# A recurrent chain of 16 chunks written out in full, with part of its VectorE work given to ScalarE

## What is computed

```
def step(M, chunk):                       # 64 tokens; 16 chunks one after the other
    eta, alpha = ...                      # means over the chunk of sigmoids
    outputs = einsum('bci,boi->bco', chunk, M)
    k_mean = (chunk / norm(chunk)).mean(axis=1)
    v_target = value_gen(outputs).mean(axis=1)
    err = v_target - einsum('boi,bi->bo', M, k_mean)
    M_new = alpha * M + eta * err[:, :, None] * k_mean[:, None, :]
    M_new = gate * M_new + (1 - gate) * M
    scale = minimum(30 / (norm(M_new) + 1e-6), 1)
    return M_new * scale, outputs
final_out = value_gen(outs)               # value_gen(y) = silu(y @ vg_w1.T) @ vg_w2.T + y
```

## Time and profile before

| | us |
|---|---|
| runs before: median of 3 (lowest to highest) | 1191.34 (1190.2 to 1191.75) |
| the profiled execution: its own time | 1186.12 |
| the profiled execution: its span, first to last instruction | 1184.1 |
| of this, from the chain's first product to the transposes after it | 909.21 to 998.88, 89.7 |
| one chunk in the chain, between the states of chunks 0 and 14 | 77.06 / 14 = 5.50 |

### The profile page before, as it was taken

One profiled execution on the slowest core, in us unless ns is written; L12 is line 12 of the kernel. 1 busy time (PEld: TensorE's weight loads), 2 busy tenths in 40 slices (PEclk: granted clock), 3 DMA queues, 4 the chain that ended last, 5 costly groups with the idle time before them and its releaser, 6 DMA issues.

```text
span 1184.1 us, 20954 instructions
## 1 busy us (share of the span) xinstructions
PE 1063.8 (90%) x5294; PEld 707.9 (60%) x5326; DVE 881.7 (74%) x2121; ACT 813.5 (69%) x1285; POOL 231.0 (20%) x328
## 2 busy tenths in 40 slices
PE   5638999999998559999999999999989888799997
PEld 2212222222322538888888888888868776677876
DVE  5863444334344669999999999999987888779997
ACT  5437999999998337777877787778762332256664
POOL 8454445445444200000000000000004111100000
PEclk9768999999999889999999999999997999699999
DMA  3455666666665137666666666676620000043231
GB/s 96 115 163 156 203 205 212 214 198 206 221 200 192 29 118 287 233 249 231 248 239 243 242 231 253 230 251 232 244 76 1 0 0 0 1 136 109 91 111 35
DMA packets 92907, 192.46 MB, mean 163 GB/s; under 512 B 9672, under 2 KB 56392, under 8 KB 82632
## 3 DMA queue, kind: packets, MB, share of 16 engines
q1 hardware_dynamic: 92880, 192.15, 48.0%
HBM read 154.03 MB, written 38.08 MB: 162 GB/s over the span
## 4 chain that ended last, share of the span: by engine, by line
PE 75%; DVE 13%; issue 4%; ACT 4%; POOL 2%; DMA 2%; DVEq 0%; ACTq 0%; SPq 0%; POOLq 0%
PE bank L1154 25%; PE bank L1167 14%; PE bank L1024 9%; PE bank L1161 8%; PE bank L1006 6%; PE bank L1009 5%; ACT ring L803 2%; PE bank L1035 1%; DVE state L1656 1%; PE bank L1255 1%; DVE ring L1396 1%; DVE xn L1346 1%; DMA ring<-c_rows 1%; DVE stats L1334 1%; PE bank L927 1%
## 5 line engine op out<-in xcount | busy, mean ns | idle before, releaser
L803 ACT ACTIVATE ring<-bank,minus_bound 128x1024 f32<-128x1024 f32 x256 | 271.3, 1111 | 30.8 <-PE bank L1009 13.5
L1154 PE MATMUL bank<-xh,w_parts 128*128 128x512 f32 x896 | 277.2, 391 | 1.9 <-DVEq L1554 1.9
L859 ACT ACTIVATE bank<-bank 128x512 f32<-128x512 f32 x320 | 186.2, 582 | 90.9 <-PE bank L1154 90.9
L1568 DVE TENSOR_TENSOR bank<-bank,ring 128x512 f32<-128x512 f32 x320 | 223.9, 700 | 29.5 <-DMA ring<-c_rows 6.6
L1167 PE MATMUL bank<-hh,w_parts 128*128 128x512 f32 x776 | 239.7, 390 | 0.0
L1560 DVE TENSOR_TENSOR hl<-bank,hh 128x512 fp32r<-128x512 f32 x321 | 218.6, 681 | 0.1
L1429 DVE TENSOR_TENSOR bank<-bank,corner 128x128 f32<-128x128 f32 x256 | 76.6, 299 | 174.4 <-PE bank L1009 145.7
L853 ACT ACTIVATE hh<-bank 128x512 fp32r<-128x512 f32 x321 | 190.4, 593 | 3.1 <-DVE bank L1568 3.0
L1154 PEld LDWEIGHTS bank<-xh,w_parts 128*128 128x128 f32 x896 | 168.0, 188 | 37.9 <-DVEq L1554 2.3
L1154 PE MATMUL bank<-xl,w_parts 128*128 128x512 f32 x448 | 174.7, 390 | 0.0
L1167 PEld LDWEIGHTS bank<-hh,w_parts 128*128 128x128 f32 x776 | 145.9, 188 | 30.7 <-ACT hh L853 0.4
(11 more groups left out here) (263 smaller groups left out, 1252.4 us busy)
## 6 DMA issues: line engine op xcount, KB each, us to landing
ring<-c_rows SPq DMA_DIRECT2D x80, 1024.0 KB, 5.1
w_parts<-w_pairs SPq DMA_DIRECT2D x160, 128.0 KB, 2.5
w_pairs<-xh SPq DMA_DIRECT2D x16, 768.0 KB, 4.4
q_stack<-q_parts SPq DMA_DIRECT2D x64, 144.0 KB
k_stack<-k_parts SPq DMA_DIRECT2D x64, 144.0 KB
w_pairs<-xl SPq DMA_DIRECT2D x16, 512.0 KB, 3.6
ring<-c_rows SPq DMA_DIRECT2D x16, 512.0 KB, 4.7
big<-in_w_exp SPq DMA_DIRECT2D x16, 384.0 KB, 4.8
```

Source lines behind the costliest of these rows:

```text
L803: act.activation(ring[:, c % RING * S:(c % RING + 1) * S], wide[c % 2][:], ACT.Exp, bias=minus_bound[:]).then_inc(exp_done, 1)
L859: act.activation(bank(4 + c % ZB), bank(4 + c % ZB), ACT.Silu).then_inc(silu_ready, 1)
L1154: ins = pe.matmul(out_, w[i], x_[j], start=start and k == 0, stop=stop and k == 2, skip_group_check=not start)
L1568: dve.tensor_tensor(bank(4 + c % ZB), bank(4 + c % ZB), cb[u][:, g * GW:(g + 1) * GW], ALU.mult).then_inc(hid_ready, 1)
```

## The change

All four loops are written out chunk by chunk, so that waits are on constants. Beside that:

- The decayed state `kept[b] = state[b] * steps[...]` is made by ACT, not by DVE, for chunk n + 1 at the end of chunk n. For chunk 0 it is made right after `steps_ready`.
- The sum of squares of batch 0 is made by ACT (`Square`), that of batch 1 stays on DVE. PE's sum waits for both.
- DVE makes both states directly after one another. Before, batch 0's squares stood between them.
- The second part of the outputs is copied out of PSUM by ACT, to `out_sum`. DVE adds the linear part and writes `memT` itself (`take_out`), and it does so for chunk n - 1 after the copy of the norm's sum in chunk n. ACT's copy to `memT` is gone.
- POOL's copy of `steps` is gone; PE and DVE read `steps`.
- Two spare products stand in each chunk, not four.
- In the last chunk the error products, the new state and its squares are left out, since nothing reads them.

```diff
-            with pool.Fori(0, NCH // 2) as i:
-                for u in range(2):
-                    n = i * 2 + u
-                    free(pool, err_psum[0], n, 1)
-                    free(pool, err_psum[1], n, 1)
-                    pool.tensor_copy(step[u][:], steps_flat[:, bass.ds(i * (2 * B * 3) + u * (B * 3), B * 3)])\
-                        .then_inc(step_ready, 1)
-                    ready(pool, norm_sq, n)
-                    pool.tensor_tensor(m_norm[:, 2, :], m_norm[:, 1, :], root[:, 0:B], ALU.pow).then_inc(norm_ready, 1)
+            for n in range(NCH):
+                pool.wait_ge(norm_sq, n + 1)
+                pool.tensor_tensor(m_norm[:, 2, :], m_norm[:, 1, :], root[:, 0:B], ALU.pow).then_inc(norm_ready, 1)
...
+            act.wait_ge(steps_ready, 1)
-            with act.Fori(0, NCH // 2) as i:
-                for u in range(2):
-                    n = i * 2 + u
-                    ready(act, scale_ready, n)
-                    for b in range(B):
-                        ready(act, mz_psum[b], n)
-                        act.activation(silu_z[b][:], bank(b)[:, 0:CH], ACT.Silu, scale=m_norm[:, 3, b:b + 1],
-                                       accum_out=h_sum[b][:]).then_inc(mz_silu[b], 1)
-                    for b in range(B):
-                        ready(act, out_taken[b], n)
-                        act.activation(memT[:, bass.ds(i * (2 * CH) + (b * S + u * CH), CH)], out_sum[b][:],
-                                       ACT.Copy).then_inc(out_copied[b], 1)
+                act.activation(kept[b], state[b][:], ACT.Copy, scale=steps[:, 0, b, 0:1]).then_inc(side_ready, 1)
+            for n in range(NCH):
+                act.wait_ge(scale_ready, n + 1)
+                for b in range(B):
+                    act.wait_ge(mz_psum[b], n + 1)
+                    act.activation(silu_z[b][:], bank(b)[:, 0:CH], ACT.Silu, scale=m_norm[:, 3, b:b + 1],
+                                   accum_out=h_sum[b][:]).then_inc(mz_silu[b], 1)
+                if n < NCH - 1:
+                    act.wait_ge(state_ready[0], n + 1)
+                    act.activation(m_sq[:, 0, :], state[0][:, 0:D], ACT.Square, accum_out=m_norm[:, 0, 0:1]).then_inc(side_ready, 1)
+                for b in range(B):
+                    act.wait_ge(out_psum[b], n + 1)
+                    act.activation(out_sum[b][:], bank(4 + b)[:, CH:2 * CH], ACT.Copy).then_inc(side_ready, 1)
+                for b in range(B if n < NCH - 1 else 0):
+                    act.wait_ge(state_ready[b], n + 1)
+                    act.activation(kept[b], state[b][:], ACT.Copy, scale=steps[:, n + 1, b, 0:1]).then_inc(side_ready, 1)
...
-                    free(pe, rows_ready, n, 1)
-                    pe.matmul(bank(6)[:, 256:256 + B], ones[:], m_norm[:, 0, :], start=True, stop=True).then_inc(norm_psum, 1)
-                    ready(pe, step_ready, n)
-                    for b in range(B):
-                        pe.matmul(bank(2 + b)[:, 0:2 * D], across(step[u][:, 3 * b + 2:3 * b + 3], P), state[b][:],
-                                  start=True, stop=True).then_inc(old_psum[b], 1)
-                    for b in range(B):
-                        free(pe, out_taken[b], n, 1)
-                        pe.matmul(bank(4 + b)[:, 0:CH], state[b][:, 0:D], chunk[b], start=True, stop=True)
-                    spare(7, 4)
-                    for b in range(B):
-                        ready(pe, mz_silu[b], n)
...
+                if n:
+                    pe.wait_ge(rows_ready, n)
+                    pe.wait_ge(side_ready, B + 5 * (n - 1) + 1)
+                pe.matmul(bank(6)[:, 256:256 + B], ones[:], m_norm[:, 0, :], start=True, stop=True).then_inc(norm_psum, 1)
+                for b in range(B):
+                    pe.matmul(bank(2 + b)[:, 0:2 * D], across(steps[:, n, b, 2:3], P), state[b][:],
+                              start=True, stop=True).then_inc(old_psum[b], 1)
+                for b in range(B):
+                    if n:
+                        pe.wait_ge(out_taken[b], n)
+                    pe.matmul(bank(4 + b)[:, 0:CH], state[b][:, 0:D], chunk[b], start=True, stop=True)
+                spare(7, 2)
+                for b in range(B):
+                    pe.wait_ge(mz_silu[b], n + 1)
+                    if n < NCH - 1:
...
-                ready(pe, out_copied[b], NCH - 1)
+                pe.wait_ge(out_taken[b], NCH)
...
-                    ready(dve, norm_psum, n)
-                    dve.tensor_copy(m_norm[:, 1, :], bank(6)[:, 256:256 + B]).then_inc(norm_sq, 1)
-                    ready(dve, step_ready, n)
-                    for b in range(B):
-                        link.sign(dve.tensor_scalar(kept[b], state[b][:], step[u][:, 3 * b:3 * b + 1], None, ALU.mult))
-                    link.wait()
-                    for b in range(B):
-                        ready(dve, old_psum[b], n)
-                        link.sign(dve.scalar_tensor_tensor(kept[b], bank(2 + b)[:, 0:2 * D], step[u][:, 3 * b + 1:3 * b + 2],
-                                                           kept[b], ALU.mult, ALU.add))
-                        if b == 0:
...
+            def take_out(n):
+                for b in range(B):
+                    dve.wait_ge(side_ready, B + 5 * n + (2 if n < NCH - 1 else 1) + b)
+                    dve.scalar_tensor_tensor(memT[:, b * S + n * CH:b * S + (n + 1) * CH], bank(4 + b)[:, 0:CH], m_norm[:, 3, b:b + 1],
+                                             out_sum[b][:], ALU.mult, ALU.add).then_inc(out_taken[b], 1)
+            for n in range(NCH):
+                dve.wait_ge(norm_psum, n + 1)
+                dve.tensor_copy(m_norm[:, 1, :], bank(6)[:, 256:256 + B]).then_inc(norm_sq, 1)
+                if n:
+                    take_out(n - 1)
+                for b in range(B):
+                    dve.wait_ge(old_psum[b], n + 1)
+                    dve.wait_ge(side_ready, 5 * n + b + 1)
+                    link.sign(dve.scalar_tensor_tensor(kept[b], bank(2 + b)[:, 0:2 * D], steps[:, n, b, 1:2], kept[b], ALU.mult, ALU.add))
+                    if b == 0:
+                        dve.wait_ge(norm_ready, n + 1)
+                        if n:
+                            dve.wait_ge(out_taken[0], n)
+                            dve.wait_ge(out_taken[1], n)
+                        link(dve.tensor_scalar(m_norm[:, 3, :], m_norm[:, 2, :], 1e-6, None, ALU.add))
+                        link(dve.reciprocal(m_norm[:, 3, :], m_norm[:, 3, :]))
+                        dve.tensor_scalar(m_norm[:, 3, :], m_norm[:, 3, :], MAX_NORM, 1.0, ALU.mult, ALU.min)\
+                            .then_inc(scale_ready, 1)
+                link.wait()
+                dve.wait_ge(scale_ready, n + 1)
+                if n < NCH - 1:
                     for b in range(B):
                         link.sign(dve.tensor_scalar(kept[b], kept[b], m_norm[:, 3, b:b + 1], None, ALU.mult))
                     link.wait()
                     for b in range(B):
-                        ready(dve, err_psum[b], n)
-                        dve.scalar_tensor_tensor(state[b][:], bank(6 + b)[:, 0:2 * D], step[u][:, 3 * b + 1:3 * b + 2],
+                        dve.wait_ge(err_psum[b], n + 1)
+                        dve.scalar_tensor_tensor(state[b][:], bank(6 + b)[:, 0:2 * D], steps[:, n, b, 1:2],
                                                  kept[b], ALU.mult, ALU.add).then_inc(state_ready[b], 1)
-                        ready(dve, state_ready[b], n)
-                        ins = dve.tensor_tensor_reduce(m_sq[:, b, :], state[b][:, 0:D], state[b][:, 0:D], 1.0, 0.0,
-                                                       ALU.mult, ALU.add, m_norm[:, 0, b:b + 1])
-                        if b == B - 1:
-                            ins.then_inc(rows_ready, 1)
-                    for b in range(B):
-                        ready(dve, out_psum[b], n)
-                        free(dve, out_copied[b], n, 1)
-                        link(dve.tensor_copy(out_sum[b][:], bank(4 + b)[:, CH:2 * CH]))
-                        dve.scalar_tensor_tensor(out_sum[b][:], bank(4 + b)[:, 0:CH], m_norm[:, 3, b:b + 1], out_sum[b][:],
-                                                 ALU.mult, ALU.add).then_inc(out_taken[b], 1)
-                assert link.n - first == per_turn, (link.n - first, per_turn)
-            link.end_loop(NCH // 2, per_turn)
+                    dve.wait_ge(state_ready[1], n + 1)
+                    dve.tensor_tensor_reduce(m_sq[:, 1, :], state[1][:, 0:D], state[1][:, 0:D], 1.0, 0.0,
+                                             ALU.mult, ALU.add, m_norm[:, 0, 1:2]).then_inc(rows_ready, 1)
+            take_out(NCH - 1)
```

More of the change, by code:

```diff
@@ L355, in build @@
         fold_ready = sem("fold_ready")
-        step_ready = sem("step_ready")
+        side_ready = sem("side_ready")
         state_ready = [sem(f"state_ready{b}") for b in range(B)]
@@ L362, in build @@
         scale_ready = sem("scale_ready")
```

(13 more changed lines are left out.)

40 lines of the change are left out of this document (4 added, 36 removed).

## The result

| | before | after |
|---|---|---|
| median of 4 runs each, us (lowest to highest) | 1190.77 (1188.25 to 1191.75) | 1172.24 (1167.51 to 1173.16) |
| the profiled execution: own time, span | 1186.12, 1184.1 | 1171.71, 1170.0 |

The ratio is 0.984, with a 95% interval of 0.9808 to 0.9871: the changed kernel is 18.5 us faster. The forecast was 1180.3 with a range of 1176 to 1187. Its sign was right and its size was not: 8.1 us too little, and the range missed the time. Of the 8.1, 7.5 are the gain (18.5 where 11.0 was forecast); the rest is the median of before, 1190.77 here and 1191.34 in the forecast.

A forecast was written before the change was run, and what follows sets the result against it. VectorE's gapless list (3.48 us) plus silu and product (1.87) bound each chunk. Fourteen chunks at 0.61 less give 8.6 us, the end 2.4, together 11.0; 1175.1 against the profiled execution, 1180.3 as a median, range 1176 to 1187.

The forecast's parts named there:

- the scale's first step, T+3.02: In each chunk, T being batch 0's state start: scale starts at T+3.02 through sum, copy and root; chunk 4.89 us.
- State 1 at T+0.50: Batch 1's state waits for its error product, about 0.5 us after the first pair, so starts at T+0.50, not T+0.73.
- The norm's copy 0.55 behind the sum: VectorE's copy of the norm's sum starts 0.55 us after PE's sum, at T+1.94; bounds 0.37 and 0.75.
- The root, 0.23 and 0.73, and the link of 0.12 to VectorE: POOL's root starts 0.23 us after the copy, takes 0.73, and VectorE follows 0.12 later (0 to 0.15).
- The other path, T+2.83: PE's old products, first there at T+2.43, then VectorE's addition: the scale's first step could start at T+2.83.
- The low end, 4.70: Shortest chunk, with sum, copy and root links short and old products deciding: 2.83 + 1.87 = 4.70 us, 11.2 us gained.
- Chunk 0, nothing is gained: First chunk: PE works off eight spare products until 909.4 us, sum, root and scale follow as before; no gain.
- The end, T+5.9: Last chunk: transposes start 5.9 us after state 14 instead of 8.32, a gain of 2.4 us.
- a gain behind the chain: Rival: PE's clock stands better behind the chain after a shorter end, 2 to 4 us more gained, 1177 us; chance 0.04.
- ScalarE's queue decides: Rival: ScalarE's operations run longer, `kept[0]` comes at T+2.83, chunk 5.1 us, time 1183.5 us; chance 0.09.
- PE's clock falls: Rival: with two fewer spare products PE's clock drops, low chunks 2.0 us longer, 1196 us with eight; chance 0.06.
- Code must be fetched: Rival: fetching the code of 16 written-out chunks stalls the chain, four stalls costing 7 us, 1187 us; chance 0.05.

The follow-up runs named there:

- the version with the outputs' part alone: Changed kernel with the decayed state and both squares back on VectorE, outputs done the new way: 5.497 us per chunk mean, thirteen at 5.39, one at 6.87.

## Why the prediction was right in kind and short in size

The step that failed is the sum of links up to the scale's first step, T+3.02. It came at T+2.65, which makes the chunk 4.52 us and not 4.89, 5.1 us over fourteen chunks. Two terms that were put at nothing, chunk 0 and the stretch behind the chain, gave 0.6 and 1.0 more, and the end 0.4.

- *VectorE's list sets the chunk, and what leaves it counts in full, until something else comes last*: right. Of the 0.98 (5.504 less 4.524), the decayed state is worth 0.53 and the square 0.34. The remaining 0.11 is what writing out the loop gives, and the outputs' part adds nothing to it.
- *State 1 at T+0.50*: it came at T+0.40 (two states in 0.88 us, each 0.48). I had read the distance of the error products' pairs; at full clock the second pair is there before VectorE has done the first state.
- *Squares and sum, T+1.39*: T+1.26. Of the 0.13 less, 0.10 is the state's and 0.03 the step's own.
- *The norm's copy 0.55 behind the sum*: 0.42 here. This is the largest mis-sized link, 0.13. The row that I leaned on, chunk 0 before, was taken with the clock at 0.50 for part of the time, and its sum took 0.53 instead of 0.38. At clock 1.00, chunk 0 of the changed kernel shows 0.44 (913.81 to 914.25). Among my bounds the low one, 0.37, was the nearer.
- *The root, 0.23 and 0.73, and the link of 0.12 to VectorE*: 0.24, 0.69 and 0.04. I had read 0.15 off a row where VectorE was busy with its own list, and had said so; I should have let that doubt pull the value down.
- *The other path, T+2.83*: the first addition came at T+2.22 and not T+2.43, the scale's step 0.43 behind it. In the changed kernel it stands right behind VectorE's two outputs; with these ahead of the copy it waited for the product and came at T+2.22 all the same, so the product too was there 0.21 earlier than I had it, 0.13 of that from the sum. Nor was there the wait for POOL that I had named as a sign: VectorE has no gap ahead of the scale's first step, only the one ahead of the norm's copy. Thus both paths came out at T+2.65, not T+3.02 and T+2.83, and the sum of the small differences is the 0.37 by which the chunk is shorter than forecast: 0.10 + 0.03 + 0.13 + 0.03 (the root) + 0.08 (the link). Times 14, that is 5.1 of the missing 7.2 us (18.2 less 11.0).
- *The last leg, 1.87 us*: 1.87 (937.83 to 939.70).
- *The low end, 4.70*: it took only the sum, copy and root links at their short ends. The old products' path, left at its middle, then decided. The state's step, common to both, had no bound at all. A low end needs every link on every path at its short end.
- *The loop's own 0.31 in every second chunk is within this*: right. Written out alone, twelve of fourteen chunks are 0.16 shorter than the mean of before, half of 0.31; the two longer ones bring the mean gain down to 0.126.
- *Chunk 0, nothing is gained*: 0.6 was. From the first product to the sum it was 0.42 instead of 0.74, since the clock was higher by then; from the sum to the scale's first step 1.41 instead of 1.69, since the decay no longer stood in VectorE's list. From there to the state both have 1.86.
- *The end, T+5.9*: T+5.52. Of this 0.37 is again the scale's earlier step.
- *Nothing behind the chain*: 1.0 us came there. The sixteen transposes took 1.94 us instead of 3.47, at the full clock. This was the rival of a gain behind the chain, with a chance of 0.04, at half of the least that it named. It isn't shown to be the change's: the old chain written out, without any other part of the change, also has them in 1.94 us, the versions with the square and with the decayed state on VectorE in 3.16 and 3.60, and the kernel before with more filler in 2.57.
- *ScalarE's queue decides*: no. `kept[0]` was there at T+1.53 and `kept[1]` at T+1.93, for additions at T+2.22 and T+3.13. The Trainium skill's figure ("ScalarE: Activation LUTs", section "Rules for kernel authors"), 0.51 for one such activation, is what one took here: 0.504. But two in a row took 0.90, and the square took 0.31 where the figure gives 0.41, so the queue as a whole was faster than by that rule. My T+2.37 for `kept[0]` by that rule left out the gaps that my own row had; with them it is T+2.42, and its reserve was 0.01. My 0.41 from the neighbouring rows was too low for one, and right for the distance of two.
- *PE's clock falls*: the clock was 1.00 in the chain, with two spares, four or none. TensorE's pause ahead of the error products was 0.19 us, not 0.5, since the chunk is shorter. The one chunk that ran at 0.50, in the version with the outputs' part alone, was 1.48 us longer, where I had priced it at 2.0.
- *Code must be fetched*: no wait of VectorE's for its own instructions is among those of the chain, and all fourteen chunks took 4.52 or 4.53. With the square on VectorE one such stop, of 0.26 us, is in the trace. *One table load*: at 913.83, and no other.
- *5.2 us from the profiled execution to the median*: by the clocks of the runs this is how early the clock fell in that execution; what sets that stays open. The profiled execution after, 1171.71, is only 0.5 below its median.

## What to carry to other kernels

When an engine's list leaves the critical path, the links between engines come to light, and a link must be read from a row where the receiver really waited and the clock was what it will be; rows in which the receiver was busy give an upper bound only, and five small excesses in a row made 0.37 us of a chunk, 5.1 in all. Compare a stage by its own marks in the trace, a chunk's length or the distance of two states, and not by one run's whole time, when work ahead of it varies by several us. Look at every chunk before you trust their mean: one chunk of 6.87 us among thirteen of 5.39 made a mean of 5.50, which would have read as a loss. Where paths are level, as the root, VectorE's list and TensorE's old product here, taking one away brings nothing (0.04 us), while an operation behind their meeting point brings all of its time (0.40).

## What the runs showed of the hardware

- The kernel before took 1181.91 to 1191.24 us in 13 runs on one chip. In the traces looked at, the moment at which TensorE's clock fell from 2.4 to 1.2 GHz lay between some 888 and some 900 us with the same order of work but for nine filler products in some, and the chain began between 907.0 and 914.6 us.
- Behind a pause of TensorE's of 1.73 us, the clock fell to 0.50 for some 6 us in one trace; in another with the same pause it stayed at 1.00.
- Start to start at full clock: TensorE's sum to VectorE's copy 0.42 us, that copy to GpSimd's root 0.24, and VectorE's next step 0.04 behind the root's end.
- Two states of 128 x 256 on VectorE, one right behind the other, took 0.88 us, and each alone 0.48. ScalarE's two copies of that shape took 0.90, and each alone 0.50.
- Two extra products of 512 columns moved the chunk by 0.01 us where the profile's busy time for them rose by 0.46: here the modelled end of a run of products was no measure of when the next could start.
